# A two-layer graph network on one core: GpSimd's memset of an idle region stands behind every second gather of source rows in place of behind each

## The chip, the cores and the metric

The kernel runs on one core of a Trainium2 chip. The metric is device time in microseconds (us), lower is better. The engines are TensorE (PE in the profile), VectorE (DVE), ScalarE (ACT), GpSimd (POOL) and SyncE (SP, which only issues DMAs here).

## What is computed

A graph has 3125 nodes with 256 features and 53125 edges, sorted by their target (`dst`). Two layers run one after the other, each on the normalised features. The first is an attention with 4 heads of rank 16, followed by a dense step; the second sums the neighbours' rows and puts the sum through a GRU cell.

```python
# layer 1 (h = relu(layernorm(x)))
ZU = jnp.einsum('nd,kdr->knr', Z, U)               # 4 heads x 16 numbers for each node
zs, zd = ZU[:, src, :], ZU[:, dst, :]              # rows of the sources, of the targets
logits = (zs * zd).sum(-1) / scale
exp_l = jnp.exp(logits - segment_max(logits, dst)[:, dst])
alpha = exp_l / (segment_sum(exp_l, dst)[:, dst] + 1e-16)
agg = segment_sum(alpha[..., None] * zs, dst)
...
x = x + relu(grad_step - ETA * LAM)                # a dense step on agg and h
# layer 2 (h = relu(layernorm(x)))
red = segment_sum(h[src] + relvectors[edge_type_16], dst)
x = x + gru_cell(red, h, w_ih, w_hh, b_ih, b_hh)
```

## The kernel before

**Windows.** The nodes are cut into 25 windows of 125. Since the edges are sorted by target, a window's edges are one run of at most 18 x 128; a window is worked on as 18 columns (`C = 18`) of 128 edges, in three chunks of 8, 8 and 2 columns (`CHUNKS`). Every engine has its own instruction stream, and all order between them is by semaphores written out by hand; no scheduler moves anything.

**The first layer's data.** The products ZU are made first, and stored in HBM as `zu_table`, 64 numbers a node. For each of the 18 columns of a window GpSimd issues one indirect DMA (line 724) that gathers 128 rows of `zu_table` by the indices in `src_col`. A window's rows land in one of three buffers `zs[t % 3]`: two lie in the tile `shared`, the third is `zs_third`, and so the profile shows them under these two names. The gathers of window t wait for `V_made`, which VectorE raises when it has weighed the rows of window t-3 (line 1083, the last reader of that buffer). Each chunk has its own semaphore in `g_zs`. All 450 gathers are issued in order, and the only other work on GpSimd among them is the memset at line 729.

**The memset.** `idle` is a region of 54 partitions x 300 numbers at the end of the tile `cnt_rows`, which nobody reads in this path. Each memset waits on the semaphore `idle_set` until the memset before it has ended, and raises it by one. No other engine waits for `idle_set`.

**The step of a window.** VectorE's `attend(t)` makes the weights of window t (`differ`, then `weigh_rows` at line 1083 after ScalarE's exponential), then the one-hot matrix of window t+1, then the logits of t+1 chunk by chunk: line 1038 waits for the chunk's gathers and for TensorE's rows of the targets (line 1804), and multiplies the two; line 1041 sums. TensorE's `attend(t)` does `target_rows(t+1)` (line 1804), the sum over edges (line 1829), the transposes of the logits, the dense step, and the part of the second layer that needs no neighbours (`own_products(t-1)`, lines 1871 to 1876). In windows 1 to 18 TensorE, VectorE and ScalarE also count pairs of nodes ahead for the second layer (`pairs_of`, line 999; `count_ahead`, line 1911; `keep_staged`, line 1570).

**The second layer.** It begins when the 25th window is through, multiplies the counts with the rows of h (lines 1947, 1948) and runs the GRU. GpSimd then only loads counts (line 745).

Of the kernel before, what the change touches and what calls it, by code (L numbers as in the profile page):

```python
# [24 lines left out]
def gnn_kernel(nc, x, edges, U, Dmat, head_w, rel, w_ih, w_hh, b_ih, b_hh, out):  # L25
# [9 lines left out]
    W, C = WINDOW, TILES  # L35
# [20 lines left out]
    with ctx:  # L56
# [3 lines left out]
        def sem(name):  # L60
            return ctx.enter_context(nc.semaphore(name))
# [45 lines left out]
        idle = cnt_rows[0:3 * C, N - 300:N]  # L107
# [183 lines left out]
        idle_set = sem("idle_set")  # L291
# [400 lines left out]
        def _(pool):  # L692
# [23 lines left out]
            def source_rows(t, i, h):  # L716

                if t in GROUP_AT:
                    pool.wait_ge(a_col, 3 * GROUP_AT[t] + 1)
                if t >= 3:  # L720
                    pool.wait_ge(V_made, t - 2 + CREDIT)
                for c, (a, b) in enumerate(CHUNKS):
                    for j in range(a, b):
                        nc.gpsimd.indirect_dma_start(  # L724
                            out=zs[t % 3][:, j * KR:(j + 1) * KR], out_offset=None, in_=zu_table,
                            in_offset=bass.IndirectOffsetOnAxis(ap=src_col[:, t, j:j + 1], axis=0),
                        ).then_inc(g_zs[t % 3][c], 16)
                        pool.wait_ge(idle_set, t * C + j + 1)
                        nc.gpsimd.memset(idle, 0.0).then_inc(idle_set, 1)  # L729

            def windowed():
                pool.sem_inc(idle_set, 1)
                pool.wait_ge(st_zu, 16 * 2 * 5)
                each_window(source_rows)
                pool.wait_ge(zd_made[2], NW)
                pool.wait_ge(st_counts, 32 * AHEAD)
                load_counts(0)
                load_counts(1)
                for t in range(2, AHEAD):
                    pool.wait_ge(sum_made, t - 1)  # L740
                    load_counts(t)
# [1370 lines left out]
```

## Time and profile before

| | |
|---|---|
| median of three runs | 1061.5 us (1060.14 to 1062.06) |
| span of the profiled execution | 1059.6 us, the only time that it has: no device time of its own stands beside the span |
| TensorE busy | 862.7 us, 81% |
| GpSimd busy | 647.8 us, 61%, nearly all before 724 us |
| VectorE busy | 631.8 us, 60% |
| ScalarE busy | 421.5 us, 40% |
| mean granted clock of TensorE | 0.833 of full speed |

The span runs from the first instruction to the last; the median of the runs is 1.9 us above it. Busy time is summed over the whole program, which has two parts of different kind: up to about 724 us GpSimd gathers and all engines work on the first layer, and from about 747 us TensorE works through the second. A line in the rows below is a line of the kernel before.

### The profile page before, as it was taken

Reading aid. Unit: us, or ns where it says so; the run is one execution under the profiler, and the core shown is the slowest. Engines: PE = TensorE matmul, PEld = TensorE weight load, DVE = VectorE, ACT = ScalarE, POOL = GpSimd, SP = SyncE. Lnnn points to the kernel's source line nnn. Section 1 sums busy time; section 2 is a strip of 40 time slices with the busy share of each in tenths; the row PEclk is TensorE's granted clock in tenths of the full one; section 3 lists DMA queues with packets and bytes.
Section 4 is the critical chain, followed back from the end, with each engine's and each line's share of the span. In section 5 each row is a group of like instructions: output and inputs, shape, how many; then the busy total and the mean of one; then the engine's idle time right before and its main releaser. Section 6 shows DMA issues by size and latency. Waiting matters only on the chain.

```text
span 1059.6 us, 14242 instructions
## 1 busy us (share of the span) xinstructions
PE 862.7 (81%) x4828; PEld 640.4 (60%) x4828; DVE 631.8 (60%) x1285; ACT 421.5 (40%) x804; POOL 647.8 (61%) x969
## 2 busy tenths in 40 slices
PE   6943688787788878787887786676999999999996
PEld 6741676565566656565665564464676676677773
DVE  5340577787888867777777764453243343388853
ACT  5423216555555555555565543341211111124441
POOL 4698888888888888888888888883001001000000
PEclk9996557787777777777787787787999999999998
DMA  9361334445455544554454553323344434421111
GB/s 196 77 156 36 74 78 120 119 119 125 116 128 130 132 123 112 129 123 125 119 129 111 120 124 89 88 51 84 95 126 141 124 116 137 124 87 49 50 51 34
DMA packets 54646, 112.99 MB, mean 107 GB/s; under 512 B 15435, under 2 KB 32968, under 8 KB 51443
## 3 DMA queue, kind: packets, MB, share of 16 engines
q1 hardware_dynamic: 34632, 81.38, 24.1%
q0 software_dynamic: 18880, 30.57, 17.5%
q8 instruction: 41, 0.67, 0.3%
q10 hardware_dynamic: 1056, 0.07, 0.1%
q14 instruction: 37, 0.30, 0.1%
HBM read 80.99 MB, written 30.86 MB: 106 GB/s over the span
## 4 chain that ended last, share of the span: by engine, by line
POOL 57%; PE 31%; issue 7%; DVE 2%; DMA 1%; SPq 1%; ACT 1%; POOLq 0%; DVEq 0%; ACTq 0%
POOL shared L724 28%; POOL cnt_rows L729 15%; POOL zs_third L724 13%; PE bank L1948 13%; PE bank L1947 6%; PE bank L1974 5%; PE bank L1975 2%; PE bank L1925 1%; PE bank L1875 1%; PE bank L1707 1%; PE bank L1971 1%; PE bank L1966 1%; DMA xs<-in_x 0%; DVE bst L885 0%; SPq L471 0%
## 5 line engine op out<-in xcount | busy, mean ns | idle before, releaser
L724 POOL DMA_INDIRECT shared<-zu_table,src_col x306 | 300.0, 980 | 51.6 <-issue 48.7
L729 POOL MEMSET cnt_rows<- 54x300 f32 x450 | 165.5, 368 | 0.3
L724 POOL DMA_INDIRECT zs_third<-zu_table,src_col x144 | 140.8, 978 | 23.0 <-issue 23.0
L999 DVE TENSOR_TENSOR setup<-iota_b,bank 128x500 bf16<-128x500 bf16 (+1 forms) x252 | 140.0, 609 | 1.1 <-PE bank L1911 0.5
L1570 ACT ACTIVATE setup<-bank 125x500 bf16<-125x500 f32 (+1 forms) x126 | 81.2, 681 | 106.5 <-PE bank L1911 70.7
L1804 PEld LDWEIGHTS bank<-zus,shared 125*128 125x128 f32 x900 | 114.0, 209 | 15.5 <-issue 14.9
L1804 PE MATMUL bank<-zus,shared 125*128 125x64 f32 x900 | 115.6, 292 | 7.8 <-ACT shared L1515 5.9
L1829 PE MATMUL bank<-layer,oh 128*125 128x84 f32 x900 | 110.1, 284 | 0.0
L1829 PEld LDWEIGHTS bank<-layer,oh 128*125 128x125 f32 x900 | 107.7, 200 | 0.1
L1911 PE MATMUL bank<-setup 128*125 128x125 bf16 x450 | 58.3, 279 | 52.0 <-DVE setup L999 42.9
L1911 PEld LDWEIGHTS bank<-setup 128*125 128x125 bf16 x450 | 48.4, 184 | 78.2 <-DVE setup L999 70.7
L1875 PE MATMUL bank<-whhT,h2T_own 128*125 128x512 f32 x100 | 90.9, 1008 | 0.0
L1193 DVE TENSOR_TENSOR layer<-bank,shared 125x512 f32<-125x512 f32 x25 | 17.3, 692 | 97.6 <-PE bank L1975 97.6
L745 POOL DMA_DIRECT2D zus<-counts_table x18 | 9.5, 534 | 106.3 <-PE bank L1948 106.1
L1948 PE MATMUL bank<-wide,zus 125*125 125x512 bf16 x208 | 70.8, 379 | 0.0
L1811 PE MATMUL bank<-ident,L 128*72 128x128 f32 x75 | 15.6, 327 | 63.5 <-DVE L L1041 43.1
L1948 PE MATMUL bank<-wide,shared 125*125 125x512 bf16 x192 | 65.6, 379 | 0.0
L1601 ACT ACTIVATE layer<-layer 125x512 f32<-125x512 f32 x25 | 15.8, 631 | 115.2 <-DVE layer L1193 115.2
L987 DVE SCALAR_TENSOR_TENSOR oh<-iota_w,win_first,bank 128x2250 f32<-128x2250 f32 x24 | 61.1, 2547 | 0.0
L1038 DVE TENSOR_TENSOR layer<-shared,bank 128x512 f32<-128x512 f32 (+1 forms) x51 | 27.9, 548 | 53.6 <-DMA shared<-zu_table,src_col 38.8
L1513 ACT ACTIVATE shared<-shared,node_id 125x2304 f32<-125x2304 int32 x25 | 55.1, 2204 | 11.9 <-issue 8.5
L745 POOL DMA_DIRECT2D shared<-counts_table x18 | 9.4, 529 | 82.3 <-PE bank L1948 82.3
(235 smaller groups left out, 1775.8 us busy)
## 6 DMA issues: line engine op xcount, KB each, us to landing
shared<-in_edges SPq DMA_DIRECT2D x25, 1125.0 KB
counts_table<-setup SPq DMA_DIRECT2D x18, 683.6 KB
own_table<-own_out SPq DMA_DIRECT2D x25, 375.0 KB
shared<-own_table SPq DMA_DIRECT2D x25, 375.0 KB
zus<-counts_table POOLq DMA_DIRECT2D x9, 683.6 KB, 5.2
shared<-counts_table POOLq DMA_DIRECT2D x9, 683.6 KB, 5.0
shared<-zu_table,src_col POOLq DMA_INDIRECT x306
h_table<-h2s SPq DMA_DIRECT2D x25, 125.0 KB
```

Of the source, the lines that this page charges most:

```text
L724: nc.gpsimd.indirect_dma_start(out=zs[t % 3][:, j * KR:(j + 1) * KR], out_offset=None, in_=zu_table, in_offset=bass.IndirectOffsetOnAxis(a ...
L729: nc.gpsimd.memset(idle, 0.0).then_inc(idle_set, 1)
L987: nc.vector.scalar_tensor_tensor(o, in0, win_first[:, bass.ds(t, 1)], col, ALU.add, ALU.is_equal).then_inc(oh_made, 1)
L999: nc.vector.tensor_tensor(chunk[n % 2][:, 0:(b - a) * W].rearrange("p (g w) -> p g w", w=W), io, ps(3, 128, at + a, at + b).unsqueeze(2).b ...
L1513: nc.scalar.activation(away, dst_bc[h], ACT.Abs, bias=node_id[0:W, t:t + 1], scale=-1.0).then_inc(away_made, 1)
L1570: nc.scalar.activation(staged.rearrange("p (a g d) -> p g a d", a=NW, g=BW)[:, a:b, :, :], ps(g % 2, W, 0, (b - a) * W).rearrange("p (g a ...
L1804: last = mm(ps(c, 128, (j - a) * KR, (j - a + 1) * KR), ohT[:, j * 128:(j + 1) * 128], zus[:, t, :], start=True, stop=True)
L1829: last = mm(ps(5, W, 0, SUMS), oh[:, h, j * W:(j + 1) * W], V[:, j, :], start=j == 0, stop=j == C - 1)
L1875: mm(ps(7, W, 0, 2 * D), rows, whhT[:, c, 0:2 * D], start=False, stop=c == CH - 1)
L1911: last = mm(ps(g % 2, W, k * W, (k + 1) * W), low_chunk[n % 2][:, k * W:(k + 1) * W], key_chunk[n % 2][:, k * W:(k + 1) * W], start=True, ...
L1947: mm(ps(bank, W, 0, D), rows, v[:, 2, :], start=False, stop=False)
L1948: last = mm(ps(bank, W, 0, 2 * D), rows, v[:, 0:2, :].rearrange("p m d -> p (m d)"), start=a == 0, stop=a == NW - 1)
```

## The change

In the loop over a window's 18 columns the memset and its wait are issued only when the column's number j is odd. So a window has nine memsets in place of 18, and the program 225 in place of 450. The wait's constant follows the new count. The gathers, their indices, buffers, waits and semaphores are the same.

```diff
@@ source_rows(t, i, h), GpSimd
                             out=zs[t % 3][:, j * KR:(j + 1) * KR], out_offset=None, in_=zu_table,
                             in_offset=bass.IndirectOffsetOnAxis(ap=src_col[:, t, j:j + 1], axis=0),
                         ).then_inc(g_zs[t % 3][c], 16)
-                        pool.wait_ge(idle_set, t * C + j + 1)
-                        nc.gpsimd.memset(idle, 0.0).then_inc(idle_set, 1)
+                        if j % 2:
+                            pool.wait_ge(idle_set, t * (C // 2) + j // 2 + 1)
+                            nc.gpsimd.memset(idle, 0.0).then_inc(idle_set, 1)
```

On GpSimd, where the path of the windows begins (the flag `general` is loaded and compared, then window 0's gathers start), this stood in a row before:

```order
L495 TENSOR_LOAD general [waits flag_ready]
L495 ISA x2
L496 COMPARE_AND_BRANCH
L724 DMA shared<-zu_table,src_col 128x64 [waits a_col,st_zu]
L729 MEMSET cnt_rows 54x300 [waits idle_set]
```

and this stands there now:

```order
L495 TENSOR_LOAD general [waits flag_ready]
L495 ISA x2
L496 COMPARE_AND_BRANCH
L724 DMA shared<-zu_table,src_col 128x64 [waits a_col,st_zu]
L724 DMA shared<-zu_table,src_col 128x64
L730 MEMSET cnt_rows 54x300 [waits idle_set]
L724 DMA shared<-zu_table,src_col 128x64 x2
```

The second gather has moved up to directly behind the first; from there on gathers go in pairs with one memset behind each pair. The second place is GpSimd's step from window 2 (`zs_third`) to window 3 (`shared`), where the wait for a free buffer, `V_made`, stands for the first time. Before:

```order
L724 DMA zs_third<-zu_table,src_col 128x64
L729 MEMSET cnt_rows 54x300 [waits idle_set]
L724 DMA shared<-zu_table,src_col 128x64 [waits V_made,a_col]
L729 MEMSET cnt_rows 54x300 [waits idle_set]
L724 DMA shared<-zu_table,src_col 128x64
```

Now:

```order
L724 DMA zs_third<-zu_table,src_col 128x64 x2
L730 MEMSET cnt_rows 54x300 [waits idle_set]
L724 DMA shared<-zu_table,src_col 128x64 [waits V_made,a_col]
L724 DMA shared<-zu_table,src_col 128x64
L730 MEMSET cnt_rows 54x300 [waits idle_set]
```

A window still ends on a memset, since it has an even number of columns, and the wait for the buffer stands at the same gather as before. No other engine's stream changes.

## Rows read from the trace of the kernel before

**Rows 1.** The page: span, and busy time, share and instructions of each engine.

```profile
span 1059.6 us, 14242 instructions
PE 862.7 (81%) x4828; PEld 640.4 (60%) x4828; DVE 631.8 (60%) x1285; ACT 421.5 (40%) x804; POOL 647.8 (61%) x969
```

**Rows 2.** The page: the chain that ended last, by engine.

```profile
POOL 57%; PE 31%; issue 7%; DVE 2%; DMA 1%; SPq 1%; ACT 1%; POOLq 0%; DVEq 0%; ACTq 0%
```

**Rows 3.** Groups of instructions: count, busy us, mean ns, idle before and releaser.

```profile
L724 POOL DMA_INDIRECT shared<-zu_table,src_col x306 | 300.0, 980 | 51.6 <-issue 48.7
L729 POOL MEMSET cnt_rows<- 54x300 f32 x450 | 165.5, 368 | 0.3
L724 POOL DMA_INDIRECT zs_third<-zu_table,src_col x144 | 140.8, 978 | 23.0 <-issue 23.0
```

**Rows 4.** Timeline of GpSimd: start us, us, line, operation [idle before, releaser].

```profile
46.87 0.97 POOL L724 DMA_INDIRECT shared<-zu_table,src_col  x1 [2.86 <-DMA zu_table<-zus]
...
107.02 0.95 POOL L724 DMA_INDIRECT zs_third<-zu_table,src_col  x1 [0.16 <-issue]
107.98 0.36 POOL L729 MEMSET cnt_rows<- 54x300 f32 x1
108.50 0.95 POOL L724 DMA_INDIRECT zs_third<-zu_table,src_col  x1 [0.16 <-issue]
...
131.57 0.95 POOL L724 DMA_INDIRECT shared<-zu_table,src_col  x1 [0.16 <-issue]
...
723.89 0.36 POOL L729 MEMSET cnt_rows<- 54x300 f32 x1
```

**Rows 5.** Waits, whole program: engine line <- releaser: us, times, longest.

```profile
DVE layer L1038 <- DMA shared<-zu_table,src_col: 38.8, 8, 8.4
DVE layer L1038 <- DMA zs_third<-zu_table,src_col: 10.5, 3, 5.5
```

**Rows 6.** Timeline of VectorE: waits for gathers, windows 18 and 24.

```profile
564.04 0.69 DVE L1038 TENSOR_TENSOR layer<-shared,bank 128x512 f32<-128x512 f32 x1 [3.25 <-DMA shared<-zu_table,src_col]
...
722.39 0.69 DVE L1038 TENSOR_TENSOR layer<-shared,bank 128x512 f32<-128x512 f32 x1 [8.35 <-DMA shared<-zu_table,src_col]
...
726.62 0.29 DVE L1038 TENSOR_TENSOR layer<-shared,bank 128x128 f32<-128x128 f32 x1 [2.82 <-DMA shared<-zu_table,src_col]
```

**Rows 7.** Timeline of VectorE: the weighing of windows 0, 19, 20 and 24.

```profile
121.00 1.35 DVE L1083 TENSOR_TENSOR layer<-shared,bank 128x1152 f32<-128x1152 f32 x1 [0.30 <-ACT bank L1465]
...
609.53 1.35 DVE L1083 TENSOR_TENSOR layer<-shared,bank 128x1152 f32<-128x1152 f32 x1 [4.34 <-ACT bank L1465]
...
627.03 1.35 DVE L1083 TENSOR_TENSOR layer<-zs_third,bank 128x1152 f32<-128x1152 f32 x1 [0.30 <-ACT bank L1465]
...
733.58 1.35 DVE L1083 TENSOR_TENSOR layer<-shared,bank 128x1152 f32<-128x1152 f32 x1 [0.30 <-ACT bank L1465]
```

**Rows 8.** Timeline of GpSimd before the windows: gathers with no memset between them.

```profile
13.42 1.23 POOL L800 DMA_INDIRECT layer<-in_edges,row_at  x1 [0.30 <-issue]
...
18.03 1.20 POOL L800 DMA_INDIRECT layer<-in_edges,row_at  x1 [0.30 <-issue]
29.23 1.21 POOL L808 DMA_INDIRECT oh<-in_edges,dst_at  x1 [10.00 <-DVE start_at L852]
30.75 1.20 POOL L808 DMA_INDIRECT oh<-in_edges,dst_at  x1 [0.30 <-issue]
...
42.81 1.20 POOL L808 DMA_INDIRECT oh<-in_edges,src_at  x1 [0.30 <-issue]
```

**Rows 9.** Timeline of GpSimd: long gathers.

```profile
59.98 1.60 POOL L724 DMA_INDIRECT shared<-zu_table,src_col  x1 [0.16 <-issue]
...
63.58 3.00 POOL L724 DMA_INDIRECT shared<-zu_table,src_col  x1 [0.16 <-issue]
```

**Rows 10.** Stretches (windows 21, 22): us, busy us by engine, clock, DMA.

```profile
634.25:661.92 27.67, 17.64 (x98) 13.05 (x97) 12.53 (x27) 9.80 (x17) 24.78 (x37) 0.75 0.37 91
661.92:688.68 26.76, 18.33 (x100) 13.37 (x98) 12.52 (x27) 9.57 (x17) 23.90 (x36) 0.74 0.38 88
```

## The prediction

> **What bounds the kernel now.** I read the page's head first. TensorE is busy for 81% of the span and GpSimd for 61% [rows 1], yet the chain that ended last lies on GpSimd for 57% and on TensorE for 31% [rows 2]. So the span has two parts with different bounds, and only the first holds gathers. The groups of instructions show what GpSimd does in its part: 450 gathers at 0.98 us (300.0 + 140.8 = 440.8 us), 450 memsets at 0.37 us (165.5 us) and 74.6 us of idle time, of which all but 2.9 us is called "issue", that is no wait for anybody [rows 3]. From the first gather at 46.87 to the end of the last memset at 724.25 are 677.4 us [rows 4], and the sum is 440.8 + 165.5 + 74.6 less the 2.9 before the first = 678.0. GpSimd never waits for a free buffer in all this time, so the gather chain runs at its own pace: 1.48 us from one gather's start to the next (107.02, 108.50), of which 0.95 is the gather, 0.36 the memset, 0.16 the gap behind it [rows 4]. A window costs 18 x 1.48 = 26.6 us, 25 of them 666; the other 11 us are gathers that took longer.
>
> Does anybody wait for this chain? VectorE's product of source and target rows does, for 38.8 + 10.5 = 49.3 us in 11 waits [rows 5]. In the timeline one of them, 3.25 us, is in window 18, and window 24 has 8.35 and 2.82 us [rows 6]; the others that matter lie between. Up to window 17 the three other engines are the slower side: the weighing of window 0 is at 121.00 and that of window 19 at 609.53, 25.7 us a window [rows 7], which starts late and catches up with the gathers' 27.1 (677.4 / 25). From window 20 on, with no counting ahead, a window needs less than the gathers take, and each of the last five is held by its rows: 733.58 - 609.53 = 124 us, 24.8 a window [rows 7]. **So what the change does to the end of the last gather, 723.88, the end of the program follows one for one**, as long as the gathers stay the slower side; a gain of more than some 30 us runs into the next limit (below), a loss runs into none.
>
> **The change, part by part.** It removes 225 memsets with their waits. The waits cost nothing themselves: a memset waits for the one before it, which has ended a gather ago. It adds nothing, and moves 225 gathers to directly behind another gather. The price is therefore one number: the distance Y from the start of one gather to the start of the next when no memset stands between. A pair costs 2 x 1.48 = 2.96 us before and Y + 1.48 after. The end moves by 225 x (Y - 1.48).
>
> Y for these gathers is not in the trace: none of the 450 stands behind another. The bounds come from the nearest rows. The lower one takes the gather's own 0.95 us [rows 4] and the gap of 0.30 us that is seen between gathers without a memset [rows 8], Y = 1.25. It takes for granted that the memset can be cut out of the time and nothing comes in its place but 0.14 us more of gap. The upper one is what the trace shows where gathers do follow each other. The ten at line 808 start at 29.23 to 42.81, nine distances of 1.509 us; those at line 800 from 13.42 to 18.03 are three of 1.537 [rows 8]. Here the gather is 1.20 and the gap 0.30. These gathers differ from those of line 724: 125 rows in place of 128, and rows of 425, 132 and 128 numbers in place of 64. The length of the row makes no difference among them, which speaks for a pace that is not set by the data.
>
> **Which value I take.** For 1.25 speaks that the first gather of line 724, whose engine had been idle for 2.86 us, took 0.97 [rows 4], while the first of line 808, after 10.00 us of idle time, took 1.21 [rows 8]: neither had anything just ahead of it, so 0.24 us of the difference belongs to the form of the gather. For 1.51 speaks that it is a distance and not a duration. Where the profile ends a gather and starts the next one is rough on this engine; the starts of a long row of gathers are not. Two very different gatherings, one with a memset and one without, come out at 1.48 and 1.51, and the memset begins the moment that the gather is put down as ended, with no idle time at all (107.02 + 0.95 = 107.97, memset at 107.98 [rows 4]), although every gather has a gap in front. That is what it looks like when the memset stands in time that the gather before it needs anyway to be done with. I take the distance, Y = 1.51: each of 225 gathers loses 0.03 us, in sum 6.75, less what the fewer rows of line 808 can't tell. I put +6 us on the profile's 1059.6 and on the median alike (the median is 1.9 us over the span): 1061.5 + 6 = 1067.5, rounded to 1067.
>
> The GPSIMD Engine Reference of the Trainium skill says in section 2.1, Instruction dispatch, that each of the engine's cores starts the next instruction as soon as it has finished its own share of the last. By that rule a memset next to a gather can run in part on cores that have nothing to do for the gather, so its row of 0.36 us overstates it; the sum by the rule alone would be no change at all. The trace agrees in that the memset starts without a gap; no run here shows the cores one by one.
>
> What stays: the number of gathers, their bytes, and everything on the other engines. The early part is not at stake, since 18 x 1.48 us after 46.87 [rows 4] the rows of window 0 are all asked for, at 74 us, and its weighing comes at 121.00 [rows 7]. Gathers can also be long for another reason, 1.60 and 3.00 us while other loads run [rows 9]; this stays as it is as long as the pace does.
>
> **Rivals.**
>
> *The memset's time is given back (faster).* Y = 1.25, a pair costs 2.73 us, a window of gathers 24.6. The gather chain would lose 225 x 0.23 = 52 us, but two limits stand in its way. First the buffers: window 3's gathers start at 131.57 [rows 4] and its buffer is free at 122.4 (121.00 + 1.35 [rows 7]), 9 us of room, which is used up by window 5; from there the gathers run in step with the weighing three windows back. Window 22 can begin when window 19 is weighed, at 610.9; three windows of 25 us (24.6 and some long gathers) end at 686, and the weighing of window 24 came 733.58 - 723.88 = 9.7 us after its last gather: 695.6. Second TensorE: windows 21 and 22 have 17.64 and 18.33 us of its work [rows 10], so with the 17.5 of window 20 and four more of 18.3 to 19 the weighing of window 24 is at 700 to 703. The later of the two holds, 31 to 33 us before 733.58; with the wait in window 18 gone too, up to 36. That gives 1026 to 1031 us, say 1028, for every Y below about 1.33, where 225 x (1.48 - Y) = 33. Above it the gain is partial. What speaks against it is the distance of 1.51; what speaks for it is the pair of first gathers.
>
> DMA: Bandwidth & Descriptors of the Trainium skill gives, in Anatomy of one DMA, about 50 ns for the sequencer's dispatch and calls the generation of descriptors small. An estimate by that page, with the gather's 0.95 us, is Y = 1.0, and it ends at the same 1028. The trace does not agree with so small a gap: it shows 0.16 and 0.30 us [rows 4, 8].
>
> *The memset is free, and Y is 1.48 (same).* A pace of 1.47 to 1.49 moves the end by 2 us at most: 1059.5 to 1063.5.
>
> *Gathers in a row are worse than the early rows show (slower, by more).* At 59.98 and 63.58 a gather took 1.60 and 3.00 us [rows 9]. If descriptors back up when gathers come closer and other DMAs run beside them, some of the 225 will be of this kind: each one in eight at 1.60 in place of 0.95 adds 28 x 0.65 = 18 us, and the time is 1080 to 1090. It decides against no change from the fourth such gather on.
>
> **How the numbers follow.** About 0.2%, 2 us, is what a measurement of this kernel can tell from no change. Likeliest case, Y of 1.49 to 1.57: 0.41, 1063.5 to 1080. Memset given back, in full or in part: 0.37 (0.31 in full, 1022 to 1034). Same: 0.15. Worse: 0.07. So faster 0.37, same 0.15, slower 0.48. The likeliest case has its own range of 1063 to 1080. The range over all has to reach into the other sign: from 1024, which leaves out about 0.05 below, to 1078, which leaves out about 0.1 above.
>
> **What the profile after would show.** The distance from an odd column's gather to the one before it is Y: read it off GpSimd's timeline. At 1.51 the last gather ends near 730 us and VectorE's waits for gathers grow from 49 to some 55 us. If the gap is 0.30 and the gather stays 0.95, the likeliest case is wrong; then GpSimd must show waits for VectorE's line 1083, VectorE's waits for gathers nearly vanish, and the last gather ends at or before 690. If the long gathers become many in windows 3 to 24, the last rival holds. The prediction is wrong as a whole if the time moves while the end of the last gather doesn't.

## The result: 1220 us, slower, and a profile that shows late signals

The changed kernel takes 1220.15 us (median of 4 runs, 1209.26 to 1223.55); the kernel before is at 1061.53 (1060.14 to 1062.06). The ratio is 1.1468, with a 95% interval of 1.1416 to 1.152. The forecast was 1067, and its range ended at 1078.

That number did not repeat. The same kernel, run later on chips 5 and 11, takes 1016.5 and 1017.4 us beside 1059.5 and 1060.0 for the kernel before: ratios 0.959 and 0.960. Which chip gave the 1220 is not recorded. So there are two things to explain, and most of the experiments were made before the second was known.

The page of the changed kernel (span; busy time, share and instructions of each engine; the chain that ended last by engine; the groups on GpSimd), against [rows 1 to 3]:

```profile
span 1221.4 us, 14017 instructions
PE 873.1 (71%) x4828; PEld 644.7 (53%) x4828; DVE 639.1 (52%) x1285; ACT 424.3 (35%) x804; POOL 565.5 (46%) x744
...
PE 53%; issue 16%; DVE 14%; another core or an unknown queue 8%; SPq 5%; ACT 2%; DMA 1%; DVEq 0%; ACTq 0%
...
L724 POOL DMA_INDIRECT shared<-zu_table,src_col x306 | 301.6, 986 | 202.1 <-DVE layer L1084 131.3
L724 POOL DMA_INDIRECT zs_third<-zu_table,src_col x144 | 138.9, 965 | 82.7 <-DVE layer L1084 50.2
L730 POOL MEMSET cnt_rows<- 54x300 f32 x225 | 83.2, 370 | 0.1
```

(Behind the edit every line's number is one higher: the weighing is L1084.) The engines do the work of before in nearly the time of before: the gathers 440.5 us, 440.8 then; TensorE 873 in place of 863. What has grown is idle time. GpSimd has left the chain, where it had 57%, and waits 131.3 + 50.2 = 181.5 us for the weighing to free a buffer, for which it had not waited once.

Timeline of GpSimd, against [rows 4]:

```profile
101.37 0.95 POOL L724 DMA_INDIRECT zs_third<-zu_table,src_col  x1 [0.16 <-issue]
102.63 0.94 POOL L724 DMA_INDIRECT zs_third<-zu_table,src_col  x1 [0.30 <-issue]
103.57 0.36 POOL L730 MEMSET cnt_rows<- 54x300 f32 x1
104.09 0.95 POOL L724 DMA_INDIRECT zs_third<-zu_table,src_col  x1 [0.16 <-issue]
...
122.62 0.37 POOL L730 MEMSET cnt_rows<- 54x300 f32 x1
146.67 0.95 POOL L724 DMA_INDIRECT shared<-zu_table,src_col  x1 [23.68 <-DVE layer L1084]
...
851.20 0.36 POOL L730 MEMSET cnt_rows<- 54x300 f32 x1
```

Y, the distance to the gather directly behind, is 102.63 - 101.37 = 1.26 us (median over the kernel 1.255): the lower bound of the forecast, not the 1.51 that it took. So the gathers did come faster, and the program became slower all the same: the last memset is at 851.20 in place of 723.89.

The waits show where (engine line <- releaser: us, times, longest). In this view "remote" stands where a signal ended the wait long after the instruction that raises it had ended, and nothing in the profile explains why so late:

```profile
DVE runs L1065 <- remote: 98.5, 20, 46.1
...
DVE den L1142 <- remote: 77.6, 20, 16.8
ACT setup L1571 <- remote: 72.3, 33, 3.9
...
ACT h2T_own L1499 <- remote: 61.4, 19, 11.2
ACT hTw_own L1538 <- remote: 59.0, 16, 4.9
```

All the rows of this kind are VectorE or ScalarE waiting for TensorE, 467 us in 167 waits. The us are the engine's whole idle time, of which a part would be there with a signal in time: the longest, 46.1, ends at 124.35, and TensorE had ended at 116.75, so it is 7.6 us late. One of them close up, in a stretch with gathers: TensorE's row, then ScalarE's, which reads what it wrote.

```profile
364.64 0.63 PE L1883 MATMUL bank<-ident,hrow_own 125*128 125x125 f32 x2
365.67 0.69 PE L1912 MATMUL bank<-setup 128*125 128x125 bf16 x4 [0.40 <-DVE setup L1000]
```

```profile
369.23 0.38 ACT L1538 ACTIVATE hTw_own<-bank 128x250 f32<-128x250 f32 x1 [4.95 <-remote]
```

TensorE is through at 365.27, ScalarE starts at 369.23: 3.96 us. The same pair is 0.04 us apart at 161.5 in this kernel and, behind the first window, everywhere in the kernel before. The profile's ends of TensorE's instructions are modelled, but TensorE was indeed through: it took up other work at 365.67. **TensorE's signals arrive late while gathers run close together.** Signals from VectorE and ScalarE to each other and to TensorE are mostly not late (0.03 to 0.14 us). Most late signals are 1 to 4 us late, and a window's chain crosses several.

The trace also holds the time at which each signal was seen, which no view prints. Here five in a row, of instructions that ended at 363.01, 364.15, 364.85, 365.27 and 366.35, are seen at 364.91, 366.35, 367.80, 369.21 and 370.64: one every 1.41 to 1.45 us, in order. So they arrive as if from a queue, each behind those ahead of it.

The weighings, against [rows 7]:

```profile
144.57 1.35 DVE L1084 TENSOR_TENSOR layer<-shared,bank 128x1152 f32<-128x1152 f32 x1 [0.30 <-ACT bank L1466]
...
343.21 1.35 DVE L1084 TENSOR_TENSOR layer<-shared,bank 128x1152 f32<-128x1152 f32 x1 [2.75 <-ACT bank L1466]
374.00 1.35 DVE L1084 TENSOR_TENSOR layer<-shared,bank 128x1152 f32<-128x1152 f32 x1 [2.72 <-ACT bank L1466]
...
896.26 1.35 DVE L1084 TENSOR_TENSOR layer<-shared,bank 128x1152 f32<-128x1152 f32 x1 [0.30 <-ACT bank L1466]
```

The first comes 23.6 us later than before, a window takes 31 (374.00 - 343.21) in place of 25.7, and the last is 896.26 - 733.58 = 162.7 us late, which is the loss of 158.6 and a few us that the second layer gives back.

### The profile page after: what moved, and what is told of

Read it like the earlier page. It is cut to its first block, busy times and chain, and to the rows that moved or that the text cites. A ratio compares the mean times of both kernels' runs of the same rounds, so it can differ in the third digit from the quotient of the medians.

```text
span 1221.4 us, 14017 instructions
## 1 busy us (share of the span) xinstructions
PE 873.1 (71%) x4828; PEld 644.7 (53%) x4828; DVE 639.1 (52%) x1285; ACT 424.3 (35%) x804; POOL 565.5 (46%) x744
## 3 DMA queue, kind: packets, MB, share of 16 engines
q0 software_dynamic: 18880, 30.57, 15.2%
## 4 chain that ended last, share of the span: by engine, by line
PE 53%; issue 16%; DVE 14%; another core or an unknown queue 8%; SPq 5%; ACT 2%; DMA 1%; DVEq 0%; ACTq 0%
PE bank L1949 11%; PE bank L1876 7%; PE bank L1948 5%; DVE setup L1000 5%; PE bank L1805 4%; PE bank L1975 4%; PE bank L1830 4%; PE bank L1912 3%; PE bank L1877 3%; PE bank L1976 2%; SPq L471 2%; DVE layer L1039 2%; SPq L473 1%; PE bank L1902 1%
## 5 line engine op out<-in xcount | busy, mean ns | idle before, releaser
L724 POOL DMA_INDIRECT shared<-zu_table,src_col x306 | 301.6, 986 | 202.1 <-DVE layer L1084 131.3
L724 POOL DMA_INDIRECT zs_third<-zu_table,src_col x144 | 138.9, 965 | 82.7 <-DVE layer L1084 50.2
L1912 PE MATMUL bank<-setup 128*125 128x125 bf16 x450 | 57.4, 275 | 115.1 <-DVE setup L1000 61.1
L1830 PE MATMUL bank<-layer,oh 128*125 128x84 f32 x900 | 115.8, 288 | 14.8 <-issue 14.6
L1912 PEld LDWEIGHTS bank<-setup 128*125 128x125 bf16 x450 | 47.4, 181 | 143.0 <-DVE setup L1000 87.5
L1830 PEld LDWEIGHTS bank<-layer,oh 128*125 128x125 f32 x900 | 111.9, 204 | 15.8 <-issue 15.8
L730 POOL MEMSET cnt_rows<- 54x300 f32 x225 | 83.2, 370 | 0.1
L1065 DVE TENSOR_TENSOR_SCAN runs<-cutf,bank 72x256 f32<-72x256 f32 x25 | 17.0, 681 | 98.5 <-remote 98.5
L1898 PE MATMUL bank<-ident,means 125*115 125x125 f32 x25 | 12.3, 492 | 64.9 <-issue 25.7
L1516 ACT ACTIVATE shared<-shared,ones 125x2304 f32<-125x2304 f32 x25 | 55.4, 2216 | 0.8
```

The costliest lines, as they stand in the source:

```text
L724: nc.gpsimd.indirect_dma_start(out=zs[t % 3][:, j * KR:(j + 1) * KR], out_offset=None, in_=zu_table, in_offset=bass.IndirectOffsetOnAxis(a ...
L1516: nc.scalar.activation(ohT, away, ACT.Relu, bias=ones[0:W, :], scale=-1.0).then_inc(oht_made, 1)
L1830: last = mm(ps(5, W, 0, SUMS), oh[:, h, j * W:(j + 1) * W], V[:, j, :], start=j == 0, stop=j == C - 1)
L1912: last = mm(ps(g % 2, W, k * W, (k + 1) * W), low_chunk[n % 2][:, k * W:(k + 1) * W], key_chunk[n % 2][:, k * W:(k + 1) * W], start=True, ...
```

## Experiments

Expectations speak of the kernels by what was known when they were written. Kernels of one heading ran on one chip, beside runs of the kernel before. "Late" is the sum of the "remote" rows of a profile's waits, so of idle time, more than the lateness alone (e2's 518.2 has 1.9 of GpSimd's own in it, the rest is for TensorE).

### Chip 1: the distance between gathers

e1 issues pairs of gathers and two memsets behind each pair:

```diff
-                        pool.wait_ge(idle_set, t * C + j + 1)
-                        nc.gpsimd.memset(idle, 0.0).then_inc(idle_set, 1)
+                        if j % 2:
+                            pool.wait_ge(idle_set, t * C + j)
+                            nc.gpsimd.memset(idle, 0.0).then_inc(idle_set, 1)
+                            pool.wait_ge(idle_set, t * C + j + 1)
+                            nc.gpsimd.memset(idle[:, 0:60], 0.0).then_inc(idle_set, 1)
```

e2 and e4 shorten the memset behind each gather to 162 and to 230 columns, and e3 has none:

```diff
-                        nc.gpsimd.memset(idle, 0.0).then_inc(idle_set, 1)
+                        nc.gpsimd.memset(idle[:, 0:162], 0.0).then_inc(idle_set, 1)
```

> Behind each pair of gathers stand two memsets in a row, 300 and 60 columns wide, so that a pair takes about as long as before (2.9 to 3.1 us) while gathers still stand directly behind each other. Theory P (pace): the other engines lose time because gathers come more often on average; at the old mean pace nothing is lost, and the time is 1055 to 1100 us, as the gather chain sets it. Theory N (neighbours): what harms is a gather directly behind a gather; then the signals of TensorE are late as in the changed kernel and the time is 1180 us or more.

> A memset behind each gather as before, but 162 columns wide in place of 300, so that the mean distance is about 1.36 us as in the changed kernel, and no gather stands behind a gather. Theory P: the time is as of the changed kernel, 1190 to 1250 us, and ScalarE's wait for TensorE's transposes at the end of a window is 3 to 4 us late as there. Theory N: no late signals, gather chain 50 us shorter, the end held by TensorE: 1025 to 1035 us.

> No memset at all, gathers 1.25 us apart. Theory P: worse than the changed kernel (1220 us), since the gathers run 0.11 us closer, 1240 us or more. Theory N: worse too, by up to the same again (450 in place of 225 neighbours), 1300 us or more. A third theory, that the waits on the semaphore idle_set hold the others up: then 1025 to 1035 us.

> A memset of 230 columns behind each gather, distance about 1.42 us. Theory P with a gradual loss: between, 1100 to 1160 us. Theory P with a threshold above this pace: the gather chain is 450 x 0.06 = 27 us shorter and the time 1035 us. Theory N: 1035 us.

Measured, beside 1103.48 us for the kernel before (1089.72 to 1117.68), which is itself 4% slower on this chip:

| | distance, us | time, us | ratio to before | late, us (waits) |
|---|---|---|---|---|
| e1 | 1.26 and 1.66 in turn | 1115.82 (1097.56 to 1134.07) | no clear difference | 267.6 (101) |
| e4 | 1.42 | 1155.59 | 1.0467 (1.0314 to 1.0621) | 415.4 (183) |
| e2 | 1.363 | 1305.33 | 1.1898 (1.1747 to 1.2049) | 518.2 (120) |
| e3 | 1.25 | 1410.05 | 1.2852 (1.2696 to 1.3009) | 791.9 (51) |

The closer the gathers, the later the signals. e2 has no gather directly behind another and is slower than e1, which has 225, so it isn't the neighbour that does it; the mean distances, 1.36 in e2 and 1.46 in e1, fit. e3 has no wait on `idle_set` at all, so those waits are not the cause. No ratio is on record for e1, of which the run of 1134.07 is the profiled one; its other run, 1097.56, lies within those of the kernel before. In e3 a window is 22.5 us of gathers, and then GpSimd waits 18 to 20 for the weighing. TensorE's sum over the edges (L1827) is through at 406.04, and its reader on VectorE starts when the gathers are over (timeline of TensorE; of GpSimd, with the last gather of a window and the first of the next; of VectorE):

```profile
404.79 1.25 PE L1827 MATMUL bank<-layer,oh 128*125 128x84 f32 x10
```

```profile
421.01 0.94 POOL L724 DMA_INDIRECT shared<-zu_table,src_col  x1 [0.30 <-issue]
440.38 1.01 POOL L724 DMA_INDIRECT shared<-zu_table,src_col  x1 [18.43 <-DVE layer L1081]
```

```profile
424.60 0.16 DVE L1139 TENSOR_SCALAR den<-bank 125x4 f32<-125x4 f32 x1 [16.70 <-remote]
```

One signal is 18.6 us late, and comes 2.65 us after the last gather has ended (421.95). In the trace it is the first of five that had been due since 406.05 to 409.02 and are seen together, from 424.57 to 425.49.

### Chip 9: the kernel before once more, a wider distance, smaller gathers

e5 is the kernel before itself. e6 has memsets of 160 and 60 columns behind each gather. e7 and e8 have no memset, and from window 3 on gather half the rows (e7, where `P` is 64 from there on and 128 before) and half of each row (e8); what isn't fetched is left as an earlier window left it. Their gathers' lines:

```diff
-                            out=zs[t % 3][:, j * KR:(j + 1) * KR], out_offset=None, in_=zu_table,
-                            in_offset=bass.IndirectOffsetOnAxis(ap=src_col[:, t, j:j + 1], axis=0),
+                            out=zs[t % 3][0:P, j * KR:(j + 1) * KR], out_offset=None, in_=zu_table,
+                            in_offset=bass.IndirectOffsetOnAxis(ap=src_col[0:P, t, j:j + 1], axis=0),
```

```diff
-                            out=zs[t % 3][:, j * KR:(j + 1) * KR], out_offset=None, in_=zu_table,
+                            out=zs[t % 3][:, j * KR:j * KR + KR // (2 if t >= 3 else 1)], out_offset=None, in_=zu_table,
```

> The kernel before, unchanged, profiled beside the three others, since its time is 1061 us in the first comparison and 1103 us in the second. If TensorE's signals are already late now and then at a distance of 1.48 us, the late ones are to be seen here wherever the time is above 1065 us; at 1061 us there are none while gathers run.

> Two small memsets (160 and 60 columns) behind each gather, distance about 1.55 us. Theory P with a limit near 1.48 us: no late signals; the gather chain alone sets the end, 450 x 0.07 = 32 us later than at 1.48 without late signals, 1093 us, which is worse than an undisturbed run of the kernel before and no worse than one of 1103 us. If a slower pace lengthens nothing, the theory that the gathers bound the last windows is wrong.

> No memset, and from window 3 on each gather fetches 64 rows in place of 128 (the other rows of the buffer keep what an earlier window left, so part of the first layer's work is left out). Each gather has half the descriptors and bytes and is itself shorter. If what delays TensorE is work for each row (descriptors), it is halved for each gather: windows of 25 to 30 us in place of 42. If it is a fixed cost of each gather, gathers now come closer still and the windows are as slow or slower for as long as gathers run.

> No memset, and from window 3 on each gathered row is 32 numbers in place of 64 (the other half keeps old values, so part of the work is left out). Number of descriptors and distance as without memsets, 1.25 us; bytes are halved. If bytes matter, the windows get shorter than 42 us; if descriptors or a fixed cost of each gather matter, the time stays at 1410 us within 1%.

The kernel before runs at 1116.33 us here (1095.89 and up, with one odd run of 2559.49). e5, its profiled run, took 1092.19 and has 189.7 us of late signals in 78 waits, at a distance of 1.475. e6, at 1.546, took 1098.14, ratio 0.9964 (0.993 to 0.9997), with a single late signal of 3.1 us: signals in time, but a slower pace (its last gather is at 760.65, 37 us behind the last memset of [rows 4]). Its ten runs lie within 4 us (1096.88 to 1100.49), where those of the kernel before, the odd one apart, spread over 33. The one late signal belongs to the time before the windows' gathers (ScalarE goes on at 43.63, the first gather of line 724 is at 46.97). So on this chip there is a distance beyond which signals are in time, between 1.475 and 1.546, and the memset of 300 columns stands just short of it.

e7 took 1409.07 us, ratio 1.2836, and e8 1414.59, 1.2886, with 774 and 728 us late. Their gathers, on GpSimd's timeline, e7 and then e8:

```profile
405.09 0.90 POOL L725 DMA_INDIRECT shared<-zu_table,src_col  x1 [0.31 <-issue]
406.30 0.90 POOL L725 DMA_INDIRECT shared<-zu_table,src_col  x1 [0.30 <-issue]
```

```profile
405.02 0.94 POOL L724 DMA_INDIRECT shared<-zu_table,src_col  x1 [0.30 <-issue]
406.26 0.94 POOL L724 DMA_INDIRECT shared<-zu_table,src_col  x1 [0.30 <-issue]
```

Half the rows take 0.04 us off the distance, half the bytes nothing, and neither brings the signals back. The distance is nearly a fixed cost per gather, and the lateness goes by the number of gathers in a time and not by their bytes. In both the queue of the gathers still moves 18880 packets, as in e3 (24.08 MB in place of 30.57), so a cost by packets isn't excluded.

### Chip 13: bursts, plain DMAs, and the pace alone

e9 puts ten memsets behind the last column and none elsewhere, so a window is 18 gathers 1.25 us apart and a break of 4 us, 1.47 to 1.49 a gather. e10 replaces the gathers by plain DMAs of fixed rows, with memsets of 300 and 60 behind. e11 has memsets of 130 and 30 behind each. e12 is e11 up to window 18 and e4 from window 19.

```diff
+                        if j == C - 1:
+                            for n in range(10):
+                                pool.wait_ge(idle_set, 10 * t + n + 1)
+                                nc.gpsimd.memset(idle, 0.0).then_inc(idle_set, 1)
```

```diff
-                        nc.gpsimd.indirect_dma_start(
+                        pool.dma_start(
+                            out=zs[t % 3][:, j * KR:(j + 1) * KR], in_=zu_table[0:128, :],
```

> 18 gathers of a window stand directly behind each other (1.25 us apart, 22.5 us), and then ten memsets of 300 columns, some 4.5 us; the mean over a window is that of the kernel before, 1.5 us. If a stretch of fast gathers harms only by its mean over tens of us, the time is as before, 1060 to 1130 us. If TensorE's signals are held up for as long as gathers come at 1.25 us and are let through in the gap only, each window is 40 us and the time near 1400 us.

> In place of the gathers GpSimd issues plain DMAs of the same size from the first 128 rows of the table (so the first layer works on wrong rows), with memsets of 300 and 60 columns behind each, so that the distance is about 1.25 us as without memsets. If what holds TensorE's signals up is a cost of any GpSimd DMA, windows are 40 us and the time is near 1400 us. If it belongs to the indirect form, the windows take the 24 us that TensorE and VectorE need and the time is 1000 to 1035 us.

> Memsets of 130 and 30 columns behind each gather, distance about 1.51 us, between the kernel before (1.48) and the one at 1.55. If the limit is below 1.51: no late signals, the gather chain sets the end, 450 x 0.035 = 16 us less than at 1.55 us, 1080 us with little spread. If the limit is above: as the kernel before on the same chip, with the same spread.

> Distance 1.51 us up to window 18, where pairs are counted ahead and TensorE signals most, and 1.42 us from window 19 on, where the gathers bound the end. If late signals need TensorE's counting beside them: 7 x 18 x 0.09 = 10 us less than the kernel at 1.51, 1070 us. If they come at any load at 1.42 us, the last windows get slower and the time is as at 1.51 us or above, 1080 to 1100 us.

Measured, beside 1061.6 us for the kernel before (1059.88 to 1063.53):

| | distance, us | time, us | ratio to before | late, us |
|---|---|---|---|---|
| e9 | 1.25, then a break | 1052.53 | 0.9909 (0.9882 to 0.9937) | 0 |
| e10 | 1.04 | 997.82 | 0.9394 (0.9372 to 0.9417) | 0 |
| e11 | 1.50 | 1078.26 | 1.0154 (1.0135 to 1.0173) | 0 |
| e12 | 1.50, then 1.42 | 1066.95 | 1.0041 (1.0023 to 1.0059) | 0 |

e11 is the pace alone: 450 x 0.02 = 9 us were to be expected from its 1.50 against 1.48, and the loss is 17; the last gather ends 14 later (738.31), and where the other 5 of those come from was not traced. e10 missed its aim, to issue plain DMAs at the distance of e3: their distance is 1.04. At first e9 and e10 read as two findings, that a break between windows saves the signals and that plain DMAs don't delay them. Both readings fell with the next chip. e12 was to tell whether late signals need TensorE's counting beside them, and can't, since nothing is late here. The trace of the changed kernel can. TensorE's counting (L1912) ends at 762 us there, and the signal that is late by most, 13.3 us, is one that was due at 839.56 (timeline of VectorE):

```profile
852.88 0.16 DVE L1142 TENSOR_SCALAR den<-bank 125x4 f32<-125x4 f32 x1 [15.02 <-remote]
```

### Chip 5: the kernels of before on another chip

e13 is e3, e14 is e9, e16 is the changed kernel. e15 is e9 with five memsets in place of ten: 1.36 us a gather over a window, as in the changed kernel.

```diff
-                            for n in range(10):
-                                pool.wait_ge(idle_set, 10 * t + n + 1)
+                            for n in range(5):
+                                pool.wait_ge(idle_set, 5 * t + n + 1)
```

> The same kernel as e3_none (no memset at all, a gather every 1.25 us), on the same chip as the three others of this group. If the slow signals belong to the spacing and not to the chip, it is slow here too, 1350 to 1420 us. If they belonged to the chip of e3_none, this one is at about 1030.

> The same kernel as e9_burst (18 gathers 1.25 us apart, then ten memsets, 1.47 to 1.49 us a gather over a window). If the break after each window is what keeps TensorE's signals in time, it is at 1050 to 1056 beside a slow e13 on this chip. If the two kernels differed only by their chips, both come out alike.

> 18 gathers 1.25 us apart, then five memsets in place of ten: a break of 2 us, 1.36 us a gather over a window, the mean spacing of the changed kernel. If what counts is the mean spacing over a window (each gather leaves some 1.45 us of work behind that the break must make up for), signals are late and the time is 1150 to 1250. If any break between windows suffices, the time is that of the second limit, 1026 to 1040.

> The changed kernel itself, beside the others on one chip: 1209 to 1224 us if chips play no part in it. It fixes what e15, with the same mean spacing but in bursts, is to be held against.

Measured, beside 1059.53 us (1058.58 to 1061.43):

| | time, us | ratio to before | late, us |
|---|---|---|---|
| e13, none | 995.3 (993.3 to 997.3) | 0.9391 (0.9337 to 0.9445) | 0 |
| e14, burst and ten | 1049.62 | 0.9903 (0.9871 to 0.9936) | 0 |
| e15, burst and five | 1007.78 | 0.9509 (0.9471 to 0.9547) | 0 |
| e16, the changed kernel | 1016.52 (1015.83 to 1017.21) | 0.9591 (0.9556 to 0.9626) | 0 |

The same program that took 1410 us takes 995. Its gathers stand 1.25 us apart as in e3, so the distance alone makes nothing late: late signals came on some chips, or at some times. GpSimd of e13 (groups, then the timeline from one window to the next) is still held by the buffer, for a moment and not for 19 us:

```profile
L724 POOL DMA_INDIRECT shared<-zu_table,src_col x306 | 296.4, 969 | 117.7 <-issue 89.0
```

```profile
318.93 0.94 POOL L724 DMA_INDIRECT shared<-zu_table,src_col  x1 [0.30 <-issue]
321.55 1.02 POOL L724 DMA_INDIRECT zs_third<-zu_table,src_col  x1 [1.67 <-DVE layer L1081]
```

The changed kernel on this chip, e16, against [rows 2, 3, 4, 7] and the profile above: chain and groups from the page; timelines of GpSimd, VectorE, TensorE and ScalarE.

```profile
span 1015.1 us, 14017 instructions
...
POOL 52%; PE 32%; issue 11%; DVE 2%; DMA 1%; SPq 1%; ACT 1%; POOLq 0%; DVEq 0%; ACTq 0%
...
L724 POOL DMA_INDIRECT shared<-zu_table,src_col x306 | 302.7, 989 | 73.9 <-issue 71.0
L724 POOL DMA_INDIRECT zs_third<-zu_table,src_col x144 | 143.6, 997 | 33.5 <-issue 33.5
L730 POOL MEMSET cnt_rows<- 54x300 f32 x225 | 83.0, 369 | 0.1
```

```profile
102.07 0.95 POOL L724 DMA_INDIRECT zs_third<-zu_table,src_col  x1 [0.16 <-issue]
103.33 0.94 POOL L724 DMA_INDIRECT zs_third<-zu_table,src_col  x1 [0.30 <-issue]
...
679.35 0.36 POOL L730 MEMSET cnt_rows<- 54x300 f32 x1
```

```profile
119.86 1.35 DVE L1084 TENSOR_TENSOR layer<-shared,bank 128x1152 f32<-128x1152 f32 x1 [0.30 <-ACT bank L1466]
...
340.74 1.35 DVE L1084 TENSOR_TENSOR layer<-shared,bank 128x1152 f32<-128x1152 f32 x1 [4.02 <-ACT bank L1466]
364.63 1.35 DVE L1084 TENSOR_TENSOR layer<-shared,bank 128x1152 f32<-128x1152 f32 x1 [4.02 <-ACT bank L1466]
...
689.00 1.36 DVE L1084 TENSOR_TENSOR layer<-shared,bank 128x1152 f32<-128x1152 f32 x1 [0.30 <-ACT bank L1466]
```

```profile
356.36 0.63 PE L1883 MATMUL bank<-ident,hrow_own 125*128 125x125 f32 x2
```

```profile
357.03 0.38 ACT L1538 ACTIVATE hTw_own<-bank 128x250 f32<-128x250 f32 x1 [1.82 <-PE bank L1883]
```

Every distance is that of the run of 1220 us, and the signal takes 0.04 us (356.99 to 357.03) in place of 3.96. A window is 23.9 us, GpSimd is the chain again, waits for no buffer, and its last memset is at 679.35 in place of 723.89.

### Chip 11: the changed kernel a third time

e17 is e16 and e18 is e14, unchanged.

> The changed kernel once more, on whatever chip it is given. The first result was 1220 us, e16 on chip 5 was 1016.5. If the chip decides, it is near one of the two, 1210 to 1230 (or more, on a chip where the kernel before is itself above 1090) or 1012 to 1020, and not between them. If the difference came from something that changes from program load to program load on one chip, any value between is possible.

> 18 gathers 1.25 us apart, then ten memsets, 1.47 to 1.49 us a gather. In e3 a stretch of gathers that began after 19 us of rest still had late signals after 8 us, so if e17 is slow on this chip and the chip decides, this one is slow as well, above 1100 us, its break of 4 us notwithstanding. If instead the break or the mean spacing is what helps, it is at 1048 to 1056 beside a slow e17. If e17 is fast, this one is at 1048 to 1056 and tells nothing more.

e17 took 1017.37 us (1016.76 to 1017.98), ratio 0.9599 (0.9571 to 0.9627); e18 took 1050.75, ratio 0.9914 (0.9885 to 0.9943), beside 1060.01. No signal is late in either. The changed kernel falls into two groups, 1220 and 1017; the burst kernel was never run where signals are late, so whether a break helps there is not known.

### What the trace of before had shown

With this in mind the waits of the kernel before, of the first profile, read differently. These are its "remote" rows:

```profile
DVE den L1141 <- remote: 8.3, 7, 1.9
...
ACT setup L1570 <- remote: 7.7, 10, 1.3
ACT h2T_own L1498 <- remote: 7.2, 6, 2.2
...
DVE runs L1064 <- remote: 3.7, 5, 1.2
...
ACT shared L1513 <- remote: 1.0, 1, 1.0
...
DVE setup L999 <- remote: 0.5, 2, 0.3
```

28.4 us in 31 waits, all for TensorE. Ten kernels profiled on chips 13, 5 and 11 have not one such row, at distances from 1.04 to 1.50. The effect was in the trace that the forecast was made from, at a distance of 1.48. It made windows longer, and the time hid it, since the gathers bound the end.

A second sign stood in the same view. VectorE and ScalarE have 50 waits there, 169.3 us, put down to "issue", that is to nothing; e16 has 2, of 1.1 us. They come from missing records: the trace of the changed kernel holds 6187 records of signals, that of e16, the same program, 13538. Every profile with late signals lacks such records (e3 5974, e13, the same program, 13371), and so does e6, which has none late while windows run (10822, where e11 with as many instructions has 14237). The ten on chips 13, 5 and 11 hold 13371 to 14300. e6 must therefore be judged without them: from the end of TensorE's instruction to the start of its reader on VectorE or ScalarE, over 433 pairs (the products with the gathered rows and `hTw_own` left out), e6 has one that is over 0.5 us late, the one at 41.9 us, the kernel before 25 and the changed kernel 139. So its signals are in time.

## Why the prediction was wrong, point by point

**The step that failed** is the sentence of "What stays", that everything on the other engines stays as it is. On the chip of the result TensorE's signals came up to 13 us late, the windows went from 25.7 to 31 to 34 us, and the time followed them. e1 to e4 show that this goes with the distance of the gathers on chip 1, e6 that signals are in time at a wider distance on chip 9, e13 and e16 that it doesn't come on another chip. No rival named it; the last one priced longer gathers, and the mean ones went from 980 to 986 ns and from 978 to 965.

**The value Y = 1.51** was wrong as well, on every chip. The argument from distances took the pace of other gathers (lines 800 and 808) for a pace of the chip. It belongs to their form: 1.20 against 0.94 for the gather, with the same gap of 0.30. The hint was there and was weighed too low: the first gathers of both kinds, with nothing ahead of them, already differed by 0.24 us [rows 4, 8]. Nor does the memset lie in time that the gather needs anyway: without it the distance falls from 1.48 to 1.255, so of the memset's 0.36 us 0.22 comes back and 0.14 goes into the wider gap. Worked out from the two rules quoted from the Trainium skill, the distance is 1.48 (GPSIMD Engine Reference, Instruction dispatch) and, as an estimate, 1.0 (DMA: Bandwidth & Descriptors, Anatomy of one DMA). The trace agrees with neither: it has 1.255, the memset isn't free and the gap is 0.30.

**The rule of the sum held where signals are in time.** "The end follows one for one": in e16 the last memset is 723.89 - 679.35 = 44.5 us earlier, and the time 1059.5 - 1016.5 = 43.0. By the groups, the memsets take 82.5 us less (165.5 to 83.0), the gaps ahead of gathers 32.8 more (71.7 to 104.5) and the gathers 5.5 more (440.8 to 446.3), 44.2 less in all. Why the gathers are longer was not traced. On the chip of the result the rule failed too: the last memset comes 127.3 us later, and the time is 158.6 longer.

**The rival "the memset's time is given back"** had the right Y and said 1026 to 1031. Its two limits did not bind: it took the weighing of window 19 at 609.53 as given [rows 7], but the windows up to there also become shorter (23.9 in place of 25.7, 579.7 by e16's weighings), and GpSimd never waited for a buffer. What held the kernel before in those windows was not its gathers: between 80 and 563 us VectorE doesn't wait for one. From its first weighing to that of window 19 it is 28.7 us longer than e16, which is about its 28.4 us of "remote" waits; that these are the cause is argued from the two numbers alone. With signals in time the gathers bind sooner: in e11, at 1.50, VectorE waits for them from 327 us on. Without any memset the end goes on falling, to 995 (e13), where windows of 23.9 us are held by the other engines, and those behind window 20 take 17.6 to 19.1, near the 18.3 to 19 of the rival's second limit. The expectations for e13 (1030) and e15 (1026 to 1040 if nothing is late) took the rival's limits over, and both came out lower, 995 and 1008.

**What the profile after was to show.** The sign for the rival came (gap 0.30, gather 0.94, waits for line 1084), and its time did not: "the last gather ends at or before 690" was 851.2 in the run of 1220 us and 679.4 in e16. "The prediction is wrong as a whole if the time moves while the end of the last gather doesn't" did not come: the end moved, by waiting.

**What stays open.** What makes signals late: no view has a row for a signal under way, and no run took TensorE's signals away from the gathers. One rival was not tested: that the recording of the profile holds the signals up. For it speaks that records of signals are missing in just the profiles of the runs with late signals, and in e6. Against it, that the other three runs of the result, 1209 to 1221 us, are as slow as the profiled one; but each has a span and a granted clock on record, so they may have been recorded in part. Whether it is the chip or the hour: the first profiles and chips 1 and 9 came before chips 13, 5 and 11, none of these five was visited twice, and the changed kernel was not run on chips 1 and 9. Whether the two traces ahead of the experiments are from one chip isn't recorded; both have late signals. Whether plain DMAs (e10) or a break (e9) avoid them can't be said from chips that have none.

## What to carry to other kernels

Before costing an edit, sum the waits whose releaser nothing in the profile explains, and ask which engine they all wait for: 28 us of them, harmless in the time, stood in the trace before an edit that brought DMA issues closer together, and 467 after it. Waits of VectorE or ScalarE that are put down to nothing belong to the same sum, since a trace can lack the record that would explain them. Take a pace only from instructions of the same form; where the form differs, the duration of one that had nothing ahead of it tells by how much. A result from one chip is one result: here the same two programs give ratios of 1.15 and 0.96, so a spacing like this one should be timed on several chips before it is kept or thrown out. On chip 5, without late signals, no memset at all is best of what was run (995 us). Where signals are late, the distances of 1.48 and 1.546, with memsets behind each gather, are the fastest that were run (with e1, at 1.26 and 1.66 in turn, not clearly slower).

## What was unexpected of the hardware

- On some chips or at some times, signals of TensorE reach VectorE and ScalarE late while GpSimd issues indirect DMAs close together, mostly 1 to 4 us (365.27 to 369.23) and in windows up to 19 (e3; one ahead of its first weighing 33), in order and, in the stretch looked at, one every 1.41 to 1.45 us. The idle time of such waits is in total 3 us at a distance of 1.546, 28 and 190 at 1.48 (two traces of the kernel before), 268 at 1.26 and 1.66 in turn, 415 at 1.42, 518 at 1.363, 792 at 1.25. On three other chips it is 0 at all distances run, 1.04 to 1.50. What makes them late is not known.
- An indirect DMA of 128 rows of 64 numbers can be issued every 1.249 us, with half the bytes every 1.249, with half the rows every 1.208; one with rows found by line 808 every 1.51.
- A plain DMA in its place occupies GpSimd for 0.53 us in place of 0.94.
